# Attention stage: keys and values fetched in half-megabyte pieces over the units, and a unit's first accumulating transfer issued ahead of an addition

## What is computed

```python
qkv = x @ w_qkv + b_qkv
q, k, v = jnp.split(qkv, 3, axis=-1)
# q and k get a rotary embedding, heads go to axis 1
attn = jnp.einsum('bhqd,bhkd->bhqk', q, k) * (1.0 / np.sqrt(hd))
attn = jax.nn.softmax(attn, axis=-1)
out = jnp.einsum('bhqk,bhkd->bhqd', attn, v)
```

## Time and profile before

| | us |
|---|---|
| Median of three runs | 3688.61 |
| The profiled execution | 3684.44 |
| Its span from first to last instruction | 3682.6 |
| Busy in the span: TensorE | 3247.0 (88%) |
| Busy: DVE / ACT / POOL | 2028.4 / 1573.8 / 1660.1 |
| Mean granted TensorE clock | 0.933 |

### The profile page before, as it was taken

One profiled execution on the slowest core, in us unless ns is written; L12 is line 12 of the kernel. 1 busy time (PEld: TensorE's weight loads), 2 busy tenths in 40 slices (PEclk: granted clock), 3 DMA queues, 4 the chain that ended last, 5 costly groups with the idle time before them and its releaser, 6 DMA issues. The chain is left out here.

```text
span 3682.6 us, 53143 instructions
## 1 busy us (share of the span) xinstructions
PE 3247.0 (88%) x15180; PEld 2087.6 (57%) x15180; DVE 2028.4 (55%) x3254; ACT 1573.8 (43%) x2848; POOL 1660.1 (45%) x732
## 2 busy tenths in 40 slices
PE   5888699999998998989999997444799999799999
PEld 5666544444444444444444443333588888688887
DVE  2878587777777776768777765434321222321222
ACT  1343226666666666657666664233211111211111
POOL 0222228877777777778877777655100000100000
PEclk9999869999999999999999998767899999899999
DMA  4444548887887878878887876654421120421210
GB/s 163 143 142 143 141 102 180 168 177 164 182 178 163 178 167 174 178 168 183 170 169 170 183 169 138 187 183 160 160 92 46 55 81 12 149 92 46 84 53 23
DMA packets 177578, 507.93 MB, mean 138 GB/s; under 512 B 25338, under 2 KB 42858, under 8 KB 143086
## 3 DMA queue, kind: packets, MB, share of 16 engines
q0 software_dynamic: 36240, 248.53, 33.1%
q1 hardware_dynamic: 130580, 233.58, 21.6%
q10 hardware_dynamic: 10512, 22.81, 1.9%
HBM read 175.18 MB, written 93.62 MB: 73 GB/s over the span
## 5 line engine op out<-in xcount | busy, mean ns | idle before, releaser
L717 DVE TENSOR_REDUCE b_mpart<-b_m 128x1 f32<-128x512 f32 x2136 | 1328.5, 684 | 480.3 <-PE b_m L767 476.0
L656 ACT ACTIVATE b_pt<-b_s 128x512 f32<-128x512 f32 x2048 | 1116.5, 596 | 625.4 <-PE b_s L792 492.7
L695 POOL TENSOR_TENSOR b_acc<-b_acc,b_pt 128x2048 f32<-128x2048 f32 x225 | 1040.4, 4624 | 352.2 <-DMA b_pt<-b_pt 350.8
L792 PE MATMUL b_s<-b_qs,b_ks 98*128 98x512 f32 x2050 | 904.2, 441 | 91.5 <-ACT b_pt L656 80.4
L792 PEld LDWEIGHTS b_s<-b_qs,b_ks 98*128 98x128 f32 x2050 | 393.7, 192 | 752.1 <-ACT b_pt L656 669.5
L767 PE MATMUL b_m<-b_ks,b_qs 96*128 96x512 f32 x2136 | 794.9, 419 | 20.9 <-issue 20.6
L844 PE MATMUL b_o<-b_pt,b_vg 128*32 128x512 f32 x4096 | 557.5, 617 | 0.0
L767 PEld LDWEIGHTS b_m<-b_ks,b_qs 96*128 96x128 f32 x2136 | 424.2, 199 | 96.4 <-DVE b_mpart L717 26.3
L1229 DVE SCALAR_TENSOR_TENSOR d_uf<-d_a,keep_chan,d_sg 128x512 f32<-128x512 f32 x128 | 96.1, 751 | 578.2 <-PE d_a L1257 578.2
L1181 POOL DMA_DIRECT2D d_raw<-in_w_fc x32 | 24.0, 755 | 592.1 <-POOLq L1106 495.7
L1200 ACT ACTIVATE d_sg<-d_g,keep_chan 128x512 f32<-128x512 f32 x128 | 88.0, 688 | 420.0 <-PE d_g L1257 420.0
(11 more groups left out here) (130 smaller groups left out, 3606.3 us busy)
## 6 DMA issues: line engine op xcount, KB each, us to landing
b_pt<-b_pt POOLq DMA_DIRECT2D x225, 1024.0 KB, 8.0
b_ks<-scratch_qk_hi SPq DMA_DIRECT2D x18, 1024.0 KB, 13.8
b_qs<-scratch_qk_hi SPq DMA_DIRECT2D x68, 256.0 KB, 6.0
scratch_qk_hi<-a_q_hi SPq DMA_DIRECT2D x64, 256.0 KB, 2.4
scratch_qk_lo<-a_q_lo SPq DMA_DIRECT2D x64, 256.0 KB, 2.8
d_h_hi<-scratch_h_hi SPq DMA_DIRECT2D x16, 1024.0 KB, 7.4
d_h_lo<-scratch_h_lo SPq DMA_DIRECT2D x16, 1024.0 KB, 9.6
d_y<-scratch_y SPq DMA_DIRECT2D x16, 1024.0 KB, 7.9
```

The lines of the kernel that those rows point to most:

```text
L656: act.activation(pt[:, kt % RING, h, :], ps_s[:, i % LEAD, :], ACT.Exp, scale=SCALE).then_inc(p_ready, 1)
L695: pool.tensor_tensor(acc[slot][:], acc[slot][:], pt[:, (2 * n + 3) % RING, :, :], ALU.add).then_inc(pool_added, 1)
L717: dve.tensor_reduce(mpart[slot][:, i // 4, i % 4:i % 4 + 1], ps_m[:, i % EARLY, :], AX.X, ALU.max).then_inc(max_done, 1)
L792: pe.matmul(ps_s[:, i % LEAD, :], ks[kslot][0:QR, h, kt * P:(kt + 1) * P], qs[qslot][0:QR, h, :], start=True, stop=True).then_inc(st_done, 1)
```

## The change

SP's large loads are cut in half. A part of the keys (32 partitions x 4 heads x 2048 keys) becomes two loads of two heads each, and the values become two loads of 8 key tiles each: 8 pieces of 512 KB for a group. They are spread over the units by `load_piece`: three steps in each unit, piece 3 * (j % 4) + step, so three pieces in units with j % 4 = 0 and 1, two with j % 4 = 2, none with 3. Step 0 is issued when the products of block 2 are done, step 1 when those of block 5 are done, step 2 after the load of the maxima. Before the loop, the first group is loaded in the same eight pieces.

On POOL, fold 0 of a unit comes ahead of addition 6 of the unit before. On ACT, a slot whose old block is even (the source of a fold) is free once the fold has landed; the odd one (its destination) still waits for the addition. Where the fold belongs to the unit before and j is 0, the even slot keeps the old wait for the addition.

```diff
-            def load_keys(G, i, r):
+            def load_keys(G, i, r, half):
                 src = qk_hi if r != 1 else qk_lo
-                sp.dma_start(f32(ks[i][r * HD:(r + 1) * HD, :, :]), src[1, G]).then_inc(k_in[i], 16)
-
-            def load_values(G, i):
-                sp.dma_start(vg[i][:], scratch["v"][G]).then_inc(v_in[i], 16)
+                heads = slice(GH // 2 * half, GH // 2 * (half + 1))
+                sp.dma_start(f32(ks[i][r * HD:(r + 1) * HD, heads, :]), src[1, G][:, heads, :]).then_inc(k_in[i], 16)
+
+            def load_values(G, i, half):
+                part = slice(NK // 2 * half, NK // 2 * (half + 1))
+                sp.dma_start(vg[i][:, part, :], scratch["v"][G][:, part, :]).then_inc(v_in[i], 16)
+
+            def load_piece(j, G, i, step):
+
+                piece = 3 * (j % 4) + step
+                if piece < 6:
+                    load_keys(G, i, piece // 2, piece % 2)
+                elif piece < 8:
+                    load_values(G, i, piece % 2)
...
                 nG, ni = (2 * pair + j // 4 + 1) % NG, (j // 4 + 1) % 2
-                if j % 4 == 0:
-                    load_keys(nG, ni, 0)
-                    load_keys(nG, ni, 1)
-                if j % 4 == 1:
-                    load_keys(nG, ni, 2)
-                if j % 4 == 2:
-                    load_values(nG, ni)
                 G, c = (2 * pair + (j + 7) // 4 + NG - 2) % NG, (j + 3) % 4
                 store_output(u, G, c)
+                sp.wait_ge(pv_done, NK * u + RING - 1 + 3)
+                load_piece(j, nG, ni, 0)
+                sp.wait_ge(pv_done, NK * u + RING - 1 + 6)
+                load_piece(j, nG, ni, 1)
                 spread_denominators(u)
                 load_maxima(u + 1, (j + 1) % 2, (j + 1) % 4)
+                load_piece(j, nG, ni, 2)
                 store_reciprocals(u, G, c)
...
-                if old >= 2:
+                if old >= 2 and old % 2 == 0:
+                    g = PAIRS * (j if kt >= RING else j - 1) + old // 2 - 1
+                    if g >= 0:
+                        act.wait_ge(pair_in[g % 2], 16 * (PAIRS * 4 * pair + g // 2 + 1 + g % 2))
+                    else:
+                        act.wait_ge(pool_added, added(u - 1, old // 2 - 1))
+                elif old >= 2:
                     act.wait_ge(pool_added, added(u if kt >= RING else u - 1, old // 2 - 1))
...
             def body(u, pair, j):
                 first_pair(u, j % 2)
+                fold_pair(u, j, pair, 0)
                 add_pair(u - 1, j - 1, pair, PAIRS - 1, (j + 1) % 2)
-                fold_pair(u, j, pair, 0)
```

More of the change, by code:

```diff
@@ L583, in _ @@
             load_queries(0, 0, 0)
-            for r in range(3):
-                load_keys(0, 0, r)
-            load_values(0, 0)
+            for half in range(2):
+                for r in range(3):
+                    load_keys(0, 0, r, half)
+            for half in range(2):
+                load_values(0, 0, half)
             sp.wait_ge(ones_ready, 1)
@@ L618, in _ @@
                 sp.wait_ge(q_in[i], 48 * (UNITS // 4 + 1))
-            sp.wait_ge(k_in[0], 48 * (NG // 2 + 1))
-            sp.wait_ge(v_in[0], 16 * (NG // 2 + 1))
+            sp.wait_ge(k_in[0], 96 * (NG // 2 + 1))
+            sp.wait_ge(v_in[0], 32 * (NG // 2 + 1))
         @block.scalar
@@ L636, in read_denominators, with slot_free @@
                 act.activation(d_sb[:], ps_d[:, 0, :], ACT.Copy).then_inc(d_read, 1)
-            def slot_free(u, kt):
+            def slot_free(u, kt, pair, j):
                 act.wait_ge(pv_done, NK * u + kt + 1)
                 old = (kt - RING) % NK
-                if old >= 2:
+                if old >= 2 and old % 2 == 0:
[5 more added lines that the diff above has]
+                elif old >= 2:
                     act.wait_ge(pool_added, added(u if kt >= RING else u - 1, old // 2 - 1))
@@ L651, in body @@
                 for kt in range(NK):
-                    slot_free(u, kt)
+                    slot_free(u, kt, pair, j)
                     for h in range(GH):
@@ L781, in operands @@
                 pe.wait_ge(q_in[j % 4], 48 * (2 * pair + j // 4 + 1))
-                pe.wait_ge(k_in[j // 4 % 2], 48 * (pair + j // 8 + 1))
+                pe.wait_ge(k_in[j // 4 % 2], 96 * (pair + j // 8 + 1))
             def turn_max(n):
@@ L840, in body @@
                         if j % 4 == 0:
-                            pe.wait_ge(v_in[kslot], 16 * (pair + 1))
+                            pe.wait_ge(v_in[kslot], 32 * (pair + 1))
                     pe.wait_ge(p_ready, STEPS * (u + 1) + GH * (kt + 1))
```

## The result

The changed kernel takes 3583.14 us (median of four, 3580.47 to 3586.58) against 3688.64 us in the same comparison: a ratio of 0.9735, 95% interval 0.9711 to 0.9758, so 2.7% faster. The forecast was 3596 us with a range from 3582 to 3645; the time lies 1.1 us above the low end. Every time here is the median of a kernel's executions; one execution of one later variant took 4129 us at a granted clock of 0.74, and its median leaves that one out.

The account below looks back on a forecast made before the run. TensorE stood behind ACT's waits for POOL's additions, laid to fold 6's late landing, plus half clock: 105.8 - 11 - 2 = 92.8, say 93; 3684.44 - 93 = 3591.4, plus 4.2 to the median, 3596 us, range 3582 to 3645.

Parts of the forecast that it names:

- What bounds the kernel: Stage B: TensorE's floor of 50.7 us a unit; 105.8 us above it from ACT's waits for POOL and half clock.
- Part 1: ACT's even slot waits for the fold's landing, not the addition: at most 3.1 us a wait, 68 us by itself.
- Part 2: Fold 0 ahead of addition 6 on POOL: cost nothing, except 2 us in units with j = 0.
- Part 3: Half-MB load pieces spread over the units: fold 6 lands 11.2 us after issue in every unit, ending unit 12's wait.
- The bounded cost: Pieces beside folds 0, 1 and 4: between nothing and 96 us, taken as 11 us over the 32 units.
- the 2 us for j = 0: Block 6 still waits for addition 6, delayed by fold 0: 0.6 us in each of 4 units.
- From span to median: Last step of the sum: the median lies 4.2 us above the profiled execution's own time, 3591.4 to 3595.6.
- Contention later in the unit: Rival, chance 0.17: pieces delay additions 3 to 5, ACT waits at blocks 7 or 11; 48 us more, 3644.
- The ring alone: Rival, chance 0.05: fold 6 lands as late as before, only the slot wait's 68 us come; 3621 us.
- The fixed part is paid: Rival, chance 0.03: 2.9 us for each added transfer paid in the open, 93 us; 3689 us.
- Slower: Rival, chance 0.05: fold 0 and step 0 make addition 6 late, block 7 waits, half clock follows; 3729 us.
- The turns gain too: Rival, chance 0.07: fewer keys beside the first fold after a loop turn save 14 us more; 3582 us.

Follow-up runs that it names:

- whole loads: The changed kernel with whole 1 MB loads, as before, at the places of steps 0 and 1, moved and not halved: 3602.98 us, ratio 0.9768.

## Why the prediction was right in size and wrong in cause

The three parts in all their combinations (us, medians; before is 3684 to 3689 in these comparisons). The last column is POOL's idle time for landings, divided by 32 units.

| order | slot wait | pieces | us | ratio | POOL idle |
|---|---|---|---|---|---|
| | | | 3684-3689 | 1 | 11.0 |
| | | x | 3690 | 1.002 | 11.6 |
| | x | | 3719 | 1.009 | 12.7 |
| | x | x | 3680 | 0.999 | 11.9 |
| x | | | 3648 | 0.989 | 5.5 |
| x | x | | 3616 | 0.982 | 6.0 |
| x | | x | 3613 | 0.980 | 4.7 |
| x | x | x | 3583 | 0.9735 | 6.4 |

Nothing without the order is faster, everything with it is. To the full kernel the order is worth 97 us, the slot wait 30, the pieces 33; by the ratios, which leave out how the kernel before differed between comparisons, it is 94, 23 and 32. The order is no single cause: alone it gives 1.1%, and the other two bring the rest only on top of it.

That the size came out right is luck. The forecast counted on all of the waits going, and they went, but by the part that it priced at nothing: without that one line the same sum would have stood beside 3680.

*What bounds the kernel.* The floor of 50.7 and the 105.8 us above it were right: 104.3 of them went. That the half clock goes with the waits was right. The step that failed is the one that followed ACT's wait back to fold 6's slow landing and stopped there. That is the last cause in unit 12, where the earlier trace rows come from, and the 22 waits were all priced as waits of this kind. Of them, 18 are at block 6 (79.7 of the 85.0 us), and in 7 of these addition 6 had waited at most 0.4 us for the landing. Unit 10 is one: POOL was at work on the first pair until 1075.17, so with the best of landings addition 6 could not have ended before 1079.7, 3 us after block 6 was due. Over stage B, fold 6's landing made 59.6 us of POOL's idle time and fold 0's 163.8; moving the loads alone took away the former and the time stayed, moving fold 0 alone brought the latter to 67.3. The sum of POOL's busy time and its waits for landings, 53.1 us a unit, stood in the profile and was not made.

*Part 1* was priced at 68 us at most by itself; it costs 0.9% by itself and gives 30 us on top of the others. The prediction named what is late next (block 7), but took the relief at block 6 as kept.

*Part 2* was "cost nothing", and that held: addition 6 was said to end 18.5 us into a unit (1027.0 in unit 9), and in unit 12 it ends at 1155.35, 18.4 us in, with block 7 due near 1157.1. In late units it ends up to 20.9 us in, and block 7 waits 0.7 and 0.8 us in two of them. But its gain was mentioned and priced at nothing, and it decides everything. That "fold 0 lands some 2 to 3 us earlier" was the mechanism: the landing then runs under addition 6, and POOL's chain is 4.6 us shorter.

*Part 3*: the landing of fold 6 came nearly in time as said, 13.2 us at most against the 12.5 given as the mark. It was thought to do nearly all; without the order it does nothing, with it 33 us. The share of the DMA engines in a unit with three pieces was said to be 0.90 and is 0.95 in unit 9 and 0.91 in unit 12.

*The bounded cost* of contention, 11 us between 0 and 96, and the 2 us for j = 0: outside the turns only 1.5 us are left, and the wait for j = 0 costs 6.7 in stage B, because it falls behind the loop's turn, where the granted clock is low as well (0.89 over unit 16). The turns' pairs came out 5.9 longer, not 110 each.

*From span to median.* The changed kernel's profiled execution took 3584.84, 6.6 us under the 3591.4 of the sum. The other 5.9 of the 12.5 us are the step to the median: before, the profiled execution lay 4.2 below its median, after, 1.7 above, and the prediction carried the 4.2 over as if it belonged to the kernel.

*The rivals.* "Contention later in the unit", priced at 48 us, did not happen: away from the turns 1.5 us are left over the floor. "The ring alone" was priced at 3621 by part 1's 68 us; order and slot wait with the loads as they were measured 3616, but the slot wait alone made the kernel slower, so that the numbers are near is chance. "The fixed part is paid" did not happen. "Slower" named POOL's order and unit 10's margin as the danger, and the sign of that mechanism was wrong. "The turns gain too" did not happen: their three pairs cost 5.9 us more than before.

## What to carry to other kernels

When one engine issues transfers and also works on what they bring, add up its busy time and its waits for landings for one period, and compare the sum with the bounding engine's period before blaming any one slow transfer. Here, with a sum above it, one faster landing brought nothing; a sum below it does not clear the engine, as the order alone showed. Then look what the engine does while a transfer is due but not issued: independent work belongs behind the issue, not before it. Relaxing a wait downstream of a late engine gained nothing by itself here. Test combinations, since edits that alone lost 0.2%, lost 0.9% and gained 1.1% gained 2.7% together.

## What the runs showed of the hardware

- A turn of the hardware loop stops ACT for 5.6 to 6.3 us in the changed kernel, a load of ACT's table (1.28 us) follows, and the granted clock is 0.93 to 0.95 in the two units around it. Two turns fewer gave 20.6 us of stage B, and 16.2 (1654.0 - 1637.8) where block 6 of j = 0 waits for the landing: 8 to 10 us a turn. Units 7 and 23, where the two turns had been, take 50.7 and 50.8 us in the body twice as long, so it showed no price of its own there.
- 0.95 of the DMA engines' time was in use in unit 9 of the changed kernel, and TensorE did not lose anything by it (busy 50.80 of 50.80 us).
- A small store feels the 1 MB fold that was issued just before it. The second of the maxima's 8 KB stores, over the 14 traces: issued less than 0.5 us after a fold's issue began, it took 1.5 us in the median to land (192 stores); 1.0 to 2.0 us after, 5.8 us (32 stores, 3.7 to 7.1); 6.0 us or more after, 1.4 us (46). In unit 4 it is 1.6 us in the changed kernel and 6.1 with whole loads.
